# Second attention of a four-layer block: the last step of the softmax reciprocal moved from VectorE to ScalarE and GpSimd

## What is computed

```python
x = x + _L0_xattn_ref(_layernorm(x), ctx_2048, ...)
x = x + _L0_ffn_ref(_layernorm(x), ...)
x = x + _L1_xattn_ref(_layernorm(x), ctx_2048, ctx_2048, gamma)
x = x + _L1_ffn_ref(_layernorm(x), ...)

def _L1_xattn_ref(q, k, v, gamma):
    ...
    qk = jnp.einsum('bhdq,bhdl->bhql', qh, kh) * scale
    sm = jax.nn.softmax(qk, axis=-1)
    ret = jnp.einsum('bhql,bhdl->bhdq', sm, vh)
    ...
    return gamma * ret
```

## Time and profile before

| what | value |
|---|---|
| median of 3 runs | 758.33 us (755.49 to 758.91) |
| profiled execution, its own time | 759.41 us |
| its span | 757.7 us |
| granted TensorE clock, mean | 0.991 |
| PE busy | 716.9 us (95%) |
| DVE busy | 571.8 us (75%) |
| ACT busy | 410.4 us (54%) |
| POOL busy | 364.5 us (48%) |
| third layer, from TensorE's first score product to its last row sums | 318.9 to 574.5 us |

### The profile page before, as it was taken

The page is one execution under the profiler, slowest core; times in us unless marked ns, Lnnn a source line. Parts: engine busy times, 40 slices in busy tenths (PEclk is TensorE's granted clock), DMA queues, the critical chain, the costliest instruction groups (busy, mean ns, idle before and its releaser), DMA issues.

```text
span 757.7 us, 14381 instructions
## 1 busy us (share of the span) xinstructions
PE 716.9 (95%) x4257; PEld 302.8 (40%) x4285; DVE 571.8 (75%) x1108; ACT 410.4 (54%) x764; POOL 364.5 (48%) x356
## 2 busy tenths in 40 slices
PE   4999999999999999899999999999998898999995
PEld 2444544444444444212222223222224555555553
DVE  4689999796876868588888898899857666555553
ACT  2555454663646556258777776777776433222221
POOL 4676555113011041355765558776675664433433
PEclk9999999999999999989999999999999999999998
DMA  8999980017264498134343344453565799998985
GB/s 304 386 142 218 293 330 0 1 39 273 100 236 176 152 311 291 46 102 107 89 118 100 98 107 113 136 158 83 171 210 115 165 184 143 133 133 128 134 113 70
DMA packets 114182, 117.51 MB, mean 155 GB/s; under 512 B 54840, under 2 KB 78264, under 8 KB 113856
## 3 DMA queue, kind: packets, MB, share of 16 engines
q1 hardware_dynamic: 103008, 94.48, 43.1%
q0 software_dynamic: 10384, 22.02, 18.0%
q10 hardware_dynamic: 720, 0.13, 0.1%
HBM read 43.61 MB, written 59.56 MB: 136 GB/s over the span
## 4 chain that ended last, share of the span: by engine, by line
PE 29%; DMA 13%; issue 8%; DVE 3%; POOL 2%; POOLq 1%; ACT 1%; DVEq 0%; ACTq 0%
PE l_b L1538 9%; PE l_sm L1557 7%; PE l_pv L1549 7%; DMA out<-t_room,t_tag 6%; DMA out<-l_pvs,t_tag 4%; PE l_a L1479 3%; DMA out<-l_sums,t_tag 2%; DVE l_negm L1771 2%; PE l_b L1492 2%; PE l_b L1529 1%; DMA out<-l_r,t_tag 1%; POOLq L1230 1%; PE l_b L1486 1%; ACT t_room L1679 1%; POOL slots_x L2127 0%
## 5 line engine op out<-in xcount | busy, mean ns | idle before, releaser
L1679 ACT ACTIVATE t_room<-l_b 128x512 f32<-128x512 f32 x256 | 139.0, 595 | 35.9 <-PE l_b L1538 33.7
L1771 DVE TENSOR_REDUCE l_negm<-l_a 128x2 f32<-128x1024 f32 x64 | 75.1, 1219 | 9.4 <-PE l_a L1479 9.2
L1157 PE MATMUL l_a<-w1h,h_stack 128*128 x312 | 76.7, 314 | 3.1 <-DVE l_stack L1210 1.7
L1186 ACT ACTIVATE l_stack<-l_stack 128x352 f32<-128x352 f32 x39 | 19.4, 497 | 105.7 <-DVE l_stack L1210 104.8
L1771 DVE TENSOR_REDUCE h_negm<-l_a 128x2 f32<-128x1024 f32 x56 | 65.9, 1220 | 9.7 <-PE l_a L1479 9.6
L1549 PE MATMUL l_pv<-t_room,l_vt 128*32 128x512 f32 x512 | 69.1, 612 | 0.1
L1557 PE MATMUL l_sm<-t_room,ones_f 128*32 128x512 f32 x512 | 68.2, 604 | 0.0
L852 PE MATMUL ps_r<-f_xt,wg 128*128 128x512 fp8e4 x256 | 65.7, 379 | 0.0
L852 PE MATMUL ps_st<-f_xt,wg 128*128 128x512 fp8e4 x256 | 65.7, 379 | 0.0
L1001 POOL TENSOR_TENSOR X<-X,f_y 128x512 f32<-128x512 f32 x16 | 20.6, 1284 | 79.3 <-ACT f_y L902 79.3
L1240 POOL DMA_INDIRECT out<-t_room,t_tag x20 | 31.7, 1586 | 47.1 <-DVE t_room L1225 34.8
(11 more groups left out here) (302 smaller groups left out, 1560.4 us busy)
## 6 DMA issues: line engine op xcount, KB each, us to landing
slots_x<-empty SPq DMA_DIRECT2D x8, 2376.0 KB, 11.0
slots_x<-empty SPq DMA_DIRECT2D x7, 2112.0 KB, 16.6
h_stack<-h_wide SPq DMA_DIRECT2D x96, 64.0 KB
l_stack<-h_wide SPq DMA_DIRECT2D x96, 64.0 KB
f_stage<-in_w SPq DMA_DIRECT2D x8, 704.0 KB, 7.2
f_stage<-in_w SPq DMA_DIRECT2D x8, 512.0 KB
h_wide<-in_ctx SPq DMA_DIRECT2D x16, 256.0 KB
l_vt<-in_ctx_t SPq DMA_DIRECT2D x16, 256.0 KB, 3.1
```

The costliest lines, as they stand in the source:

```text
L1157: mm = pe.matmul(self.HP[i % 2][:, 0:self.H], T.xt[i % T.AHEAD][:, xp * self.FC + f, :], self.w1[wp][:, bass.ds(e, 1), f * self.H:(f + 1) ...
L1679: act.activation(weights_at(u, c, h)[:, :], B[t % 2][:, :], ACT.Exp, scale=SCALE).then_inc(b_ok, 1)
L1771: dve.tensor_reduce(negm[u % 2][:, 2 * half:2 * half + 2, j], A[half][:, :, :], AX.X, ALU.max, negate=True)\
```

## The change

The Newton step is split in two for units 0 to 13. ScalarE makes sr = sr/4 - 1/2 in place (`complements`), which is (sr - 2)/4, after the weights of cycle 7 and ahead of `turned_out`. GpSimd multiplies pvs by it (`complemented`), ahead of `add`. The factor 4 is put into the scale of `result`, so there are two of these constants, -gamma and -4 gamma. Units 14 and 15 keep VectorE's fused step.

```diff
--- before.py
+++ after.py
@@ -1321,7 +1321,7 @@
         PT = [[T.room[:, (HU * r + h) * D:(HU * r + h + 1) * D] for h in range(HU)] for r in range(RING)]
         pvs = [sb(f"pvs{k}", [P, D]) for k in range(2)]
         sums, r0, sr = (sb(n, [P, D]) for n in ("sums", "r0", "sr"))
-        gam, neg_gam = sb("gam", [P, 1]), sb("neg_gam", [P, 1])
+        gam, neg_gam = sb("gam", [P, 1]), sb("neg_gam", [P, 2])
 
         gw, gb = sb("gw", [P, FC, E]), sb("gb", [P, 2, E])
         rst6, rmv, rveps, rrstd = sb("rst6", [P, 6]), sb("rmv", [P, 2]), sb("rveps", [P, 1]), sb("rrstd", [P, 1])
@@ -1387,7 +1387,7 @@
         a_ps, max_ok = F.a_ps, F.max_ok
         b_ps, b_ok = sem("bps"), sem("bok")
         pv_ps, sum_ps, pv_ok, sums_ok = (sem(n) for n in ("pvps", "sumps", "pv", "sums"))
-        ln_ok, r0_ok, sr_ok, vr_ok, ng_ok = (sem(n) for n in ("ln", "r0", "sr", "vr", "ng"))
+        ln_ok, r0_ok, sr_ok, vr_ok, ng_ok, comp_ok = (sem(n) for n in ("ln", "r0", "sr", "vr", "ng", "comp"))
         tx_ok, res_ok = sem("tx"), sem("res")
         w_in, const_ok, start_ok = sem("w"), sem("const"), sem("start")
         rstat_ok, raggr_ok, rveps_ok, rrstd_ok, xn_ok = (sem(n) for n in ("rstat", "raggr", "rveps", "rrstd", "xn"))
@@ -1679,10 +1679,11 @@
                 act.activation(weights_at(u, c, h)[:, :], B[t % 2][:, :], ACT.Exp, scale=SCALE).then_inc(b_ok, 1)
 
             def result(u):
+                k = 1 if u < NU - 2 else 0
                 act.wait_ge(pv_ps, TC * u + TC)
-                act.wait_ge(ng_ok, 1)
+                act.wait_ge(ng_ok, 2)
                 wait(act, res_ok, u - 1)
-                act.activation(pvs[u % 2][:, :], PV[:, :], ACT.Identity, scale=neg_gam[:, 0:1]).then_inc(pv_ok, 1)
+                act.activation(pvs[u % 2][:, :], PV[:, :], ACT.Identity, scale=neg_gam[:, k:k + 1]).then_inc(pv_ok, 1)
 
             def totals(u):
                 act.wait_ge(sum_ps, TC * u + TC)
@@ -1697,6 +1698,10 @@
             def first_reciprocals(u):
                 act.wait_ge(ln_ok, u + 1)
                 act.activation(r0[:, :], r0[:, :], ACT.Exp, scale=-1.0).then_inc(r0_ok, 1)
+
+            def complements(u):
+                act.wait_ge(sr_ok, u + 1)
+                act.activation(sr[:, :], sr[:, :], ACT.Identity, bias=neg_half[:, 0:1], scale=0.25).then_inc(comp_ok, 1)
 
             def turned_hidden(i):
                 ht, from_ps = tiles.turned(act, i)
@@ -1725,6 +1730,9 @@
                             for n in range(3):
                                 if u == BATCHES[n][-1] + 4:
                                     gate_weights(n)
+                    if u and u < NU - 1 and i == 7:
+                        complements(u - 1)
+                    if u >= 2:
                         if i == 7:
                             turned_out(u - 2)
             result(NU - 1)
@@ -1976,7 +1984,8 @@
             for j in range(EARLY):
                 maxima(1, j)
             dve.wait_ge(gam_ok, 16)
-            dve.tensor_scalar(neg_gam[:, :], gam[:, :], -1.0, None, ALU.mult).then_inc(ng_ok, 1)
+            for k, factor in enumerate((-1.0, -4.0)):
+                dve.tensor_scalar(neg_gam[:, k:k + 1], gam[:, :], factor, None, ALU.mult).then_inc(ng_ok, 1)
             F.queries(dve, X, 2)
             for u in range(NU):
                 if u + 1 < NU:
@@ -2007,7 +2016,7 @@
                     F.statistics(dve, X, u + 3)
                 if u + 2 < NU:
                     maxima(u + 2, 0)
-                if u:
+                if u == NU - 1:
                     normalise(u - 1)
                 if u + 2 < NU:
                     maxima(u + 2, 1)
@@ -2105,6 +2114,11 @@
                 pool.wait_ge(pv_ok, u + 1)
                 pool.tensor_tensor(pvs[u % 2][:, :], pvs[u % 2][:, :], r0[:, :], ALU.mult).then_inc(vr_ok, 1)
 
+            def complemented(u):
+                pool.wait_ge(comp_ok, u + 1)
+                pool.wait_ge(vr_ok, u + 1)
+                pool.tensor_tensor(pvs[u % 2][:, :], pvs[u % 2][:, :], sr[:, :], ALU.mult).then_inc(tx_ok, 1)
+
             def add(u):
                 pool.wait_ge(tx_ok, u + 1)
                 pool.tensor_tensor(X[:, u, :], X[:, u, :], pvs[u % 2][:, :], ALU.add).then_inc(res_ok, 1)
@@ -2165,6 +2179,7 @@
                                pattern=[[1, E], [-1, E]], channel_multiplier=0).then_inc(const_ok, 1)
             for u in range(NU):
                 if u >= 2:
+                    complemented(u - 2)
                     add(u - 2)
                 if u + 2 < NU:
                     queries(u + 2)
```

## The result

| what | before | after |
|---|---|---|
| median | 758.91 us (7 runs, 755.49 to 760.48) | 764.73 us (7 runs, 761.62 to 765.70) |
| after / before | | 1.0072, 95% interval 1.0054 to 1.0089 |
| profiled execution, its span | 759.41, 757.7 us | 764.73, 763.0 us |
| granted TensorE clock, mean | 0.991 | 0.991 |

The account below looks back on a forecast made before the run. TensorE's own list was taken to set the pace in units 2 to 7, so a faster VectorE gives nothing there. Terms of -0.1, 0, 1.0, 1.0 and 0.7 made +2.6 us on the 758.33 median: 760.9 us, range 756.8 to 765.0.

Parts of the forecast that it names:

- likeliest case: Whole kernel: no change that can be told, within 0.5%, leaning to slower; chance 0.62, of which the forecast itself 0.40.
- ScalarE's new step: Ahead of L1668 at unit ends: the step of 0.69 us fits ScalarE's idle gap of 0.71 us and costs nothing.
- The rival on this gap: ScalarE's step takes clearly more than its 0.71 us gap; at 1.0 us, 4.2 us lost, 765.1 us; chance 0.12.
- What is removed: Fourteen fused steps leave VectorE; gain of 0.1 us in unit 8, where TensorE was late for VectorE; ends 0 and 0.8.
- GpSimd's new step is free in an ordinary unit: GpSimd's product of 1.28 us costs nothing there, since GpSimd's waits of together 1.97 us cover it.
- The rival of the shared road in every unit: GpSimd's pair delays VectorE's queries, costing 0.2 to 0.4 us in each of 14 units; 764.5 us; chance 0.18.
- Unit 11: VectorE's small step behind the queries waits for GpSimd's shifted add, so maxima come late: loss 1.0 us, ends 0 and 1.3.
- Unit 14: L1872 or what follows waits for a second GpSimd instruction, with no room at TensorE: loss 1.0 us, ends 0 and 1.3.
- Unit 15: Product delays VectorE's chain by 1.28 us, less some 0.8 us if L1912's wait vanishes: loss 0.7 us, ends 0 and 1.3.
- The sign that I had named: Last unit: its sr comes 0.5 to 1.3 us later against TensorE's last row sums if the forecast is right.
- The sum: Whole kernel: -0.1 + 0 + 1.0 + 1.0 + 0.7 = +2.6 us; the terms' ends together give -0.8 to +3.9.
- two slower rivals: ScalarE's step not fitting its gap (765.1 us, chance 0.12); shared GpSimd and VectorE road in every unit (764.5 us, chance 0.18).

Follow-up runs that it names:

- Experiment 9: Kernel before plus ScalarE's new step into an unused tile in the same fourteen units: 760.38 us beside 760.06, ratio 1.0004.
- experiment 3: Changed kernel, but units 9 and 13 keep VectorE's fused step, so 12 of 14 units stay changed: 760.67 us, ratio 1.0005 to the kernel before.
- 6: Kernel before plus an unused GpSimd product ahead of the add at the starts of units 11 and 15 only: 764.64 us, ratio 1.0068.
- experiment 10: Kernel before plus an unused GpSimd product ahead of each of fourteen adds, VectorE's fused step kept: 766.61 us, ratio 1.0067.
- experiment 8: Kernel before with VectorE's early table and its meeting table moved ahead of unit 13's row statistics in unit 15: 761.66 us, ratio 1.0020.
- 12: Kernel before with VectorE's early meeting table split in two halves, moved behind unit 14's fused step and ahead of unit 15's row statistics: 764.27 us, ratio 1.0052.
- experiment 4: Changed kernel with GpSimd's product and add moved from a unit's start to the end of the unit before, ahead of the transfers: 764.52 us, ratio 1.0067.
- experiments 1: Changed kernel, but unit 13 keeps VectorE's fused step, so GpSimd's product is gone from unit 15's start: 761.32 us beside 760.00, ratio 1.0012.

## Why the prediction was right in its range and wrong in its likeliest case

- **ScalarE's new step, at nothing:** right. It takes 0.724 us where I took 0.69, and the gap was 0.71, yet nothing is late. Its span overlaps that of the weights ahead of it: in unit 5 they end at 411.18, it starts at 411.06 and ends at 411.78, so it fills 0.60 us of the gap. Experiment 9 has all fourteen for a ratio of 1.0004. I had written that no row has this exact form, and that was wrong: an Identity with a constant per row, from SBUF to SBUF and of this size, stands in the first layer of the kernel before, at 0.722 us.

```profile
L372 ACT ACTIVATE w1h<-w1h x8: 712/722/741, 38.3 to 155.0; 128x512 f32<-128x512 f32 x8
```

The Trainium skill's page "ScalarE: Activation LUTs", section "What ACT_TABLE_LOAD costs", makes it 0.71 (an estimate), also nearer than my 0.69. The rival on this gap fell with it; its point of decision, "clearly more than 0.71", was not reached.
- **What is removed, -0.1:** right, as far as so little can be told. In experiment 3 twelve fused steps are gone and the ratio is 1.0005. The period to unit 8 is 16.46 or 16.47 us in all eight traces without fused steps there. Where they stay it is 16.70 to 16.76 in three (before, 6, 10) and 16.46 to 16.48 in three (8, 9, 12), so 0.1 us is gained in the mean.
- **GpSimd's new step is free in an ordinary unit:** right. The periods of units 3 to 7 are 15.69 us in every trace. The rival of the shared road in every unit is refuted by experiments 3 and 10.
- **Unit 11, +1.0 (0 to 1.3):** the first trace shows 1.6, above its upper end; over seven traces with and six without, 0.8. The mechanism is the one forecast, the query step and the score step each behind a GpSimd instruction. TensorE's `a_quad` waits 0.81 and 0.74 us there, where I had named about 1.
- **Unit 14, +1.0:** too much. Its period is 16.68 us against 16.39, +0.3, and this repeats; over units 12 to 15 the gains and losses cancel. The blocks did grow (0.78 us for L1879 and 1.30 for the pair of L1882, where the kernel before has 0.94 and 0.30), but only 0.3 of these 0.8 us reached TensorE.
- **Unit 15, "So 0.5 to 1.3 us reach the experts' tiles. I take 0.7":** this is the step that failed. It is 3.0 us on VectorE's chain and 2.5 at TensorE. The sign that I had named, the sr of unit 15 against TensorE's last row sums, is 3.04 us later and not 0.5 to 1.3. I let the chain shift rigidly by the product's length, and even took off 0.8 us for a block that it would escape. It shifted by 1.5, and the shift brought its small steps under other GpSimd instructions, where they lost 1.5 more. I had looked at the one block that could vanish (L1912's 0.98, and it did: its step takes 0.16 us now) and not asked which steps would come to stand there instead. L1932 came under the GpSimd instruction that L1912 had met and took 1.21 us, and L1937 came under the pair of products. I also took it that a block lasts no longer than one GpSimd instruction. My upper end of 1.3 came from that; the lower one, start-up stalls that swallow the delay, did not happen either.
- **The sum and the case:** +2.6 forecast, +5.5 measured by the ratio, of which the traces give 1.1 net before unit 15 and 2.5 to 3.0 there. Each term was bounded by one product's length, so the highest sum, +3.9, could not reach it. The range held 764.73 only because it reached up to the two slower rivals, and neither of them is what happened. That the range held is luck. The likeliest case, within 0.5%, had a chance of 0.62 and did not come true: 0.72% and 0.61% were measured. The shared road itself is the mechanism, at two places, a little at a third, and not in every unit: the 3.21 us row is a VectorE step with two SBUF inputs, and it ends within 0.03 us of GpSimd's product. The Trainium skill's page "SBUF — State Buffer", section "Who interferes with whom", says that a VectorE instruction with two SBUF inputs contends with a GpSimd instruction that reads SBUF, and that the loser is blocked for the whole of the other's instruction. The row agrees in that it ends with GpSimd's. It goes beyond it in two ways: it had begun 0.67 us ahead of the first product, and it was held over both.

**What stays open:** why experiment 4's order makes ScalarE wait 2.48 us, what makes the stack's transfer late, and where in the experts' tiles the last 1 to 1.5 us of the trace arise.

## What to carry to other kernels

A step handed to an engine with idle time is free only where that engine's next wait is longer than the step; look for the few places where it is not (here 3 of 14, one of them worth only 0.3 us, behind transfers that the engine issues itself), and leave the step where it was there. Where a delayed instruction stands at the head of a long in-order chain, don't carry the delay through as a constant: lay the shifted chain beside the other engine's timeline and see what each small step now meets. And time freed on an engine that nobody waits for is worth nothing: 12 of the 14 moves together changed the time by a ratio of 1.0005.

## What the runs showed of the hardware

A blocked VectorE step can stay blocked over more than one GpSimd instruction. The 128 x 8 step started at 568.41, while GpSimd was issuing a transfer, and ended with the second of the two products behind it, 3.21 us later; this repeats as 3.21, 3.22, 3.23, 3.21 and 3.22 us in five traces. In experiment 8 the same is seen with one instruction behind the transfer: a 128 x 8 step started at 558.20, in a transfer's issue, and ended at 560.20, with the add that ended at 560.18.

A step that starts while the first of two back-to-back instructions is under way can come through when that one ends, or stay blocked over both. In the kernel before (first two lines) it came through after 1.33 us, and the same in experiments 1 and 3 (1.31 us). In unit 14 of experiment 10 (the other lines) it took 2.17 us and ended with the second:

```profile
567.16 1.33 DVE L1924 TENSOR_TENSOR l_over<-l_score,l_mine 128x80 f32<-128x80 f32 x1
567.07 1.27 POOL L2104 TENSOR_TENSOR l_sr<-l_sums,l_r 128x512 f32<-128x512 f32 x1 [0.65 <-issue]
...
545.36 2.17 DVE L1871 TENSOR_TENSOR l_score<-l_counts,l_score 128x16 f32<-128x16 f32 x1
544.98 1.29 POOL L2169 TENSOR_TENSOR l_extra<-X,l_pvs 128x512 f32<-128x512 f32 x1
546.21 1.27 POOL L2110 TENSOR_TENSOR X<-X,l_pvs 128x512 f32<-128x512 f32 x1
```

What decides between the two was not tried. It is not whether the step began ahead of the pair, though the five long blocks of unit 15 all did.
